# Graph and expert layer on one core: row statistics moved to ScalarE, a spread tile built on ScalarE, 448 tiles sorted and 336 scattered

## The reference, cut to what matters

```
h   = layernorm(x)                            # no weights, eps 1e-5
in_ = segment_mean((h @ W_in.T + b_in)[src], dst)
out = segment_mean((h @ W_out.T + b_out)[dst], src)
gi  = concat(in_, out) @ W_ih.T + b_ih;  gh = h @ W_hh.T + b_hh
r, z = sigmoid(i_r + h_r), sigmoid(i_i + h_i);  n = tanh(i_n + r * h_n)
x   = x + (1 - z) * h + z * n
x   = x + mixture(layernorm(x))               # 6 experts, top 2, three layers each
```

## Time and profile before

| | us |
|---|---|
| median of 3 runs | 3228.31 (3223.29 to 3228.78) |
| the profiled execution | 3225.96 |
| its span | 3224.2 |
| busy in the span: PE / VectorE / ScalarE / POOL | 2485.8 / 2135.0 / 836.3 / 2275.8 |
| POOL's scatters L390, 384 | 392.9 |
| POOL's gathers L423, 784 + 784 | 787.5 + 771.8 |

### The profile page before, as it was taken

The page is one execution under the profiler, slowest core; times in us unless marked ns, Lnnn a source line. Parts: engine busy times, 40 slices in busy tenths (PEclk is TensorE's granted clock), DMA queues, the critical chain, the costliest instruction groups (busy, mean ns, idle before and its releaser), DMA issues. The chain is left out here.

```text
span 3224.2 us, 68778 instructions
## 1 busy us (share of the span) xinstructions
PE 2485.8 (77%) x14180; PEld 1527.8 (47%) x14181; DVE 2135.0 (66%) x7172; ACT 836.3 (26%) x1328; POOL 2275.8 (71%) x2224
## 2 busy tenths in 40 slices
PE   4506699948888888788885888888888888488885
PEld 2202355524444444444442555555555555377774
DVE  8878999757777777777773666666666766622221
ACT  0030366512222222222220111111111111144443
POOL 3177777767777777777775777777777776167785
PEclk9957999979999999999997999999989999699998
DMA  2040000043333333333332444444444444135454
GB/s 77 17 122 9 1 1 0 0 142 107 109 109 109 107 107 107 102 103 107 106 107 83 128 127 128 127 127 129 128 127 124 134 125 119 34 66 79 78 80 53
DMA packets 167884, 293.80 MB, mean 91 GB/s; under 512 B 46611, under 2 KB 112916, under 8 KB 167830
## 3 DMA queue, kind: packets, MB, share of 16 engines
q0 software_dynamic: 109056, 235.68, 28.6%
q10 hardware_dynamic: 38566, 36.42, 3.4%
q1 hardware_dynamic: 20208, 21.15, 2.1%
HBM read 250.60 MB, written 42.49 MB: 91 GB/s over the span
## 5 line engine op out<-in xcount | busy, mean ns | idle before, releaser
L423 POOL DMA_INDIRECT ring<-split_rows,live x784 | 787.5, 1004 | 250.7 <-issue 234.6
L423 POOL DMA_INDIRECT over<-split_rows,gather_row x784 | 771.8, 984 | 238.7 <-issue 234.1
L1564 PE MATMUL bank<-over,over 128*128 (+1 forms) x4728 | 862.2, 334 | 10.4 <-DVE over L961 5.3
L1564 PEld LDWEIGHTS bank<-over,over 128*128 (+1 forms) x4728 | 455.9, 98 | 351.7 <-issue 122.9
L390 POOL DMA_INDIRECT list<-sort,sort x384 | 392.9, 1023 | 238.8 <-issue 124.9
L1638 PE MATMUL bank<-over,dense 128*128 x980 | 291.6, 399 | 150.3 <-SPq L518 75.9
L957 DVE TENSOR_SCALAR over<-iota_cols,live,live 128x128 f16 x1564 | 394.9, 317 | 1.0 <-issue 0.7
L1638 PE MATMUL bank<-ring,dense 128*128 x980 | 284.8, 392 | 115.2 <-issue 66.9
L1639 PE MATMUL bank<-ones_col,dense 128*128 128x1 f16 x1960 | 330.6, 169 | 0.0
L578 ACT ACTIVATE over<-live,live 128x788 f16 x245 | 222.2, 946 | 322.3 <-PE bank L1564 186.4
L1638 PEld LDWEIGHTS bank<-over,dense 128*128 x980 | 98.4, 100 | 313.6 <-issue 231.3
(11 more groups left out here) (296 smaller groups left out, 3674.6 us busy)
## 6 DMA issues: line engine op xcount, KB each, us to landing
ring<-split_rows,live POOLq DMA_INDIRECT x784
over<-split_rows,gather_row POOLq DMA_INDIRECT x784, 2.8
dense<-in_x ACTq DMA_DIRECT2D x52, 128.0 KB
dense<-in_edge_means ACTq DMA_DIRECT2D x52, 128.0 KB
routed_rows<-dense ACTq DMA_DIRECT2D x25, 264.0 KB
norm<-in_x SPq DMA_DIRECT2D x10, 640.0 KB, 5.6
split_rows<-norm SPq DMA_DIRECT2D x10, 640.0 KB, 4.0
in_edge_means<-dense ACTq DMA_DIRECT2D x50, 128.0 KB
```

Source lines behind the costliest of these rows:

```text
L423: g.indirect_dma_start(out=rings[d][:, i % ring_slots[d], :], out_offset=None, in_=table[:], in_offset=bass.IndirectOffsetOnAxis(ap=gather ...
L1564: ins = t.matmul(bank[h][:, 0:HS + 1], rows_(half), slots(h), start=False, stop=False, skip_group_check=True)
```

## The change

- **Sizes.** 448 tiles are sorted instead of 400, so that 336 are scattered.
- **Statistics on ScalarE.** ScalarE sums each row with an accumulating Identity (scale -1/256) and its squared distances with an accumulating Square, group by group, while VectorE runs `positions(0)`. SP loads x a first time for that, right behind the edges.
- **One chain for all tiles.** `row_scales` on VectorE computes all inverse roots at once, on 51 columns, and from them `rstd_plus`, `rstd_big`, `mean_scaled` and `mean_big`; the kernel before made two of these at the border to direction 1.
- **Rows on ScalarE.** SP loads x a second time; ScalarE makes rows times 2048 with one Identity a tile and rounds them. VectorE subtracts (`low_rows`), straight into fp16, within `positions(1)`: five groups after counting groups 4, 6, 8, 10, 12 and five after pairs of buckets 1, 3, 5, 7, 9. The scaling pass of ScalarE (L558) is gone. The high half is now 2048 times as large and the low half unscaled, so the mean uses one factor `1 / (2048 count)`, and one multiplication a bucket is gone.
- **Spread tile.** POOL makes it with one column per bucket; ScalarE copies it out to 128 columns each. `iota_half` is made by VectorE.
- **Order.** The fold's bias products come first and PE waits for their copy only; the weights' copies are waited for after the counting of direction 1. The loops of `positions` on VectorE are written out, and their increments of `turn` are gone. Several buffers lie elsewhere.

```diff
-SORTED_TILES = 400
+SORTED_TILES = 448
+COUNT_LOW = (4, 6, 8, 10, 12)
+PLACE_LOW = (1, 3, 5, 7, 9)
...
-            g.memset(spread_row, 0.0).then_inc(S["spread_ready"], 1)
+            g.memset(spread_base[:], 0.0).then_inc(S["spread_ready"], 1)
...
+            for s_ in range(2, LN_GROUPS):
+                sp.wait_ge(S["ln_stats"], s_ - 1)
+                sp.dma_start(ln_x[s_ % 2], x_b[s_]).then_inc(ln_in[s_ % 2], 16)
             for k in range(2):
+                sp.wait_ge(S["ln_stats"], LN_GROUPS - 1 + k)
                 sp.dma_start(ln_x[k], x_b[k]).then_inc(ln_in[k], 16)
+            for s_ in range(LN_GROUPS):
+                if s_ + 2 < LN_GROUPS:
+                    sp.wait_ge(S["h_ready"], s_ + 1)
+                    sp.dma_start(ln_x[s_ % 2], x_b[s_ + 2]).then_inc(ln_in[s_ % 2], 16)
+                sp.wait_ge(S["split_ready"], s_ + 1)
+                sp.dma_start(table_b[s_], ln_split[s_ % 2]).then_inc(store_landed[s_ % 2], 16)
+                sp.wait_ge(store_landed[s_ % 2], (s_ // 2 + 1) * 16)
+                sp.sem_inc(S["table_stored"], 1)
...
+            act.wait_ge(S["spread_ready"], 3)
+            a.copy(spread_row, spread_base[:].rearrange("p (b o) -> p b o", o=1).to_broadcast([P, NB, P])
+                   ).then_inc(S["spread_ready"], 1)
+            def ln_sums(s_):
+                k = s_ % 2
+                act.wait_ge(ln_in[k], (s_ // 2 + 1) * 16)
+                for t_ in range(LB):
+                    col = s_ * LB + t_
+                    ins = a.activation(ln_h[k][:, t_, :], ln_x[k][:, t_, :], ACT.Identity, scale=-1.0 / D,
+                                       accum_out=neg_mean[:, col:col + 1])
+                ins.then_inc(S["ln_mean"], 1)
+                act.wait_ge(S["ln_mean"], s_ + 1)
+                for t_ in range(LB):
+                    col = s_ * LB + t_
+                    ins = a.activation(ln_h[k][:, t_, :], ln_x[k][:, t_, :], ACT.Square, bias=neg_mean[:, col:col + 1],
+                                       accum_out=square_sum[:, col:col + 1])
+                ins.then_inc(S["ln_stats"], 1)
+            def ln_rows(s_):
+                k = s_ % 2
+                act.wait_ge(ln_in[k], (LN_GROUPS // 2 + s_ // 2 + 1) * 16)
+                if s_ >= 2:
+                    act.wait_ge(S["table_stored"], s_ - 1)
+                for t_ in range(LB):
+                    col = s_ * LB + t_
+                    ins = a.activation(ln_h[k][:, t_, :], ln_x[k][:, t_, :], ACT.Identity,
+                                       scale=rstd_big[:, col:col + 1], bias=mean_big[:, col:col + 1])
+                ins.then_inc(S["h_ready"], 1)
+                act.wait_ge(S["h_ready"], s_ + 1)
+                a.copy(ln_split[k][:, :, 0:D], ln_h[k]).then_inc(S["hi_ready"], 1)
...
+            def row_scales():
+                v.wait_ge(S["ln_stats"], LN_GROUPS)
+                inverse_root(step, rstd[:], square_sum[:], root_a[:], root_b[:], D)
+                e.tensor_scalar(rstd_plus[:], rstd[:], 1.0, None, ALU.add)
+                e.tensor_scalar(rstd_big[:], rstd[:], LO_SCALE, None, ALU.mult)
+                step(e.tensor_tensor(mean_scaled[:], neg_mean[:], rstd[:], ALU.mult))
+                e.tensor_scalar(mean_big[:], mean_scaled[:], LO_SCALE, None, ALU.mult).then_inc(S["rows_scaled"], 1)
+            def low_rows(s_):
+                k = s_ % 2
+                v.wait_ge(S["hi_ready"], s_ + 1)
+                e.tensor_tensor(ln_split[k][:, :, D:2 * D], ln_h[k], ln_split[k][:, :, 0:D], ALU.subtract
+                                ).then_inc(S["split_ready"], 1)
...
+                    e.tensor_scalar(iota_half, iota_cols[:], -0.5, None, ALU.add).then_inc(S["half_ready"], 1)
...
             positions(0)
-            layer_norm()
+            row_scales()
             positions(1)
```

More of the change, by code:

```diff
@@ L164, in gnn_moe_program @@
         raw_list = list_at
+        late = at["live"]
         step_gap = carve("live", [NS])
@@ L180, in gnn_moe_program @@
         at["norm"] = at["sort"]
-        assert at["sort"] <= LIVE - sort_words
         ln_x = [carve("norm", [LB, D]) for _ in range(2)]
[L183 to L189, removed]
+        assert at["norm"] <= LIVE - sort_words
+        late_at = region_at + 4 * late
+        ln_h = [over(late_at + 4 * k * LB * D, [LB, D]) for k in range(2)]
+        ln_split = [over(late_at + 4 * (2 + k) * LB * D, [LB, 2 * D], F16) for k in range(2)]
+        assert late + 4 * LB * D <= at["live"]
         gather_row = [gather_row_0, sb("gather_row_1", [P, NS], I32)]
         receiver = [receiver_0, sb("receiver_1", [P, NS], F32)]
-        moments = sb("moments", [P, NB + 1, 2], F32)
-        rstd = sb("rstd", [P, NB + 1], F32)
+        neg_mean, square_sum, rstd, rstd_plus, rstd_big, mean_scaled, mean_big, root_a, root_b = [
+            sb(n, [P, NB + 1], F32) for n in ("neg_mean", "square_sum", "rstd", "rstd_plus", "rstd_big", "mean_scaled",
+                                              "mean_big", "root_a", "root_b")]
+        spread_base = sb("spread_base", [P, NB], F16)
         ring_at = -(-nc.sbuf_base // 32) * 32
@@ L465, in _ @@
             sp.dma_start(key, edges).then_inc(S["edges_in"], 16)
+            x_b = x[0:NP, :].rearrange("(s t p) d -> s p t d", t=LB, p=P)
+            table_b = table.rearrange("(s t p) d -> s p t d", t=LB, p=P)
+            for k in range(2):
+                sp.dma_start(ln_x[k], x_b[k]).then_inc(ln_in[k], 16)
             sp.wait_ge(S["consts"], N_CONSTS)
@@ L561, in _ @@
+            for s_ in range(LN_GROUPS):
+                ln_sums(s_)
             act.wait_ge(S["fold_summed"], 1)
+            a.copy(gate_bias[0:2, 0:2 * D], banks[0][0:2, 0:2 * D])
+            a.copy(gate_bias[0:2, 2 * D:G3], banks[1][0:2, 0:D]).then_inc(S["bias_folded"], 1)
+            act.wait_ge(S["fold_summed"], 2)
             for m in range(4):
-                a.copy(w_gate[:, m, 0:2 * D], banks[m][:, 0:2 * D])
-                a.copy(w_gate[:, m, 2 * D:G3], banks[4 + m // 2][:, m % 2 * D:m % 2 * D + D])
@@ L565, in _ @@
-            a.copy(gate_bias[0:2, 0:2 * D], banks[6][0:2, 0:2 * D])
-            a.copy(gate_bias[0:2, 2 * D:G3], banks[7][0:2, 0:D]).then_inc(S["fold_done"], 1)
+                a.copy(w_gate[:, m, 0:2 * D], banks[2 + m][:, 0:2 * D])
+                ins = a.copy(w_gate[:, m, 2 * D:G3], banks[6 + m // 2][:, m % 2 * D:m % 2 * D + D])
+            ins.then_inc(S["fold_done"], 1)
+            act.wait_ge(S["rows_scaled"], 1)
+            for s_ in range(LN_GROUPS):
+                ln_rows(s_)
             def hi_mean_step(q, k):
@@ L873, in onehot @@
                                     ).then_inc(S["onehot_ready"], 1)
-                with v.Fori(0, COUNT_GROUPS // 2) as r:
-                    for g_ in range(2):
-                        v.wait_ge(S["onehot_used"], r * 2 + (u0 + g_ + 1))
-                        for k in range(GROUP):
-                            i = g_ * GROUP + k
-                            onehot(bass.ds(r * (2 * GROUP) + i, 1), i, iota_down)
-                v.wait_ge(S["onehot_used"], u0 + COUNT_GROUPS)
-                for b in range(COUNT_GROUPS // 2 * 2 * GROUP, NB):
-                    onehot(slice(b, b + 1), b % (2 * GROUP), iota_down)
+                for g_ in range(COUNT_GROUPS):
+                    v.wait_ge(S["onehot_used"], u0 + g_ + 1)
+                    for b in range(g_ * GROUP, min(g_ * GROUP + GROUP, NB)):
+                        onehot(slice(b, b + 1), b % (2 * GROUP), iota_down)
+                    if d == 1 and g_ in COUNT_LOW:
+                        low_rows(COUNT_LOW.index(g_))
                 v.wait_ge(S["onehot_used"], u0 + COUNT_GROUPS + 2)
@@ L1502, in fold_weights @@
                                        start=(n_ == 0), stop=(n_ == 3))
+                ins.then_inc(S["fold_summed"], 1)
+                for m in range(4):
+                    a_, c = m // 2, m % 2
+                    for o, lo_, hi_ in ((banks[2 + m][:, 0:2 * D], 0, 2 * D),
+                                        (banks[6 + m // 2][:, m % 2 * D:m % 2 * D + D], 2 * D, G3)):
+                        for k in range(2):
+                            ins = t.matmul(o, w_conv[:, 2 * a_ + k, c * P:c * P + P], w_ih_raw[:, 2 * a_ + k, lo_:hi_],
+                                           start=(k == 0), stop=(k == 1))
                 ins.then_inc(S["fold_summed"], 1)
```

148 lines of the change are left out of this document (34 added, 114 removed).

## The result

| | before | changed |
|---|---|---|
| median, us | 3228.55 (4 runs, 3223.29 to 3236.39) | 3135.11 (4 runs, 3125.23 to 3139.17) |
| ratio | | 0.9704, 95% interval 0.9674 to 0.9734 |
| profiled execution / its span | 3225.96 / 3224.2 | 3125.23 / 3123.1 |
| first scatter / decoding starts | 141.38 / 663.55 | 114.50 / 571.96 |
| PE's last step of the sort begins | 636.16 | 554.62 |

The forecast was 3147 in 3132 to 3165.

The account below looks back on a forecast made before the run. POOL's scatter chain was taken to bound the start of the gathers. Scatters starting 17.9 us earlier (16.4 - 0.5 + 2) and 48 fewer of them bring the decoding 79 us earlier: 3225.96 - 79 = 3147 us, range 3132 to 3165.

Parts of the forecast that it names:

- What bounds: Before the gathers, POOL's scatter chain is later than VectorE's and PE's by 26 us; through the gathers, POOL's issue rate.
- (1) Spread tile: At the start of POOL's chain, moving the wide spread tile off POOL frees VectorE's first operations: net 16.4 us.
- (2) Unrolled place loop: In the list positions before the first scatter, writing out the loop and dropping empty increments saves 2 us (0 to 4).
- (3) Scatters: On POOL up to the decoding, 48 scatters fewer; the remaining ones take 456.1 us, 1.358 each.
- VectorE's and PE's chain: Positions, row scales and sort: PE ends at 572.0, staying ahead of the decoding at 584.0.
- The new wait: In the second positions, VectorE waits for ScalarE's high parts: 4.6 us in the counting, none in the placing.
- rival with 10.1 us a group: High part, subtraction, store and load take 10.1 us a group, VectorE's chain ends last: 3166 us, chance 0.14.
- Sums on ScalarE: Row sums and squares beside the first positions take about 55 us, done near 75, hidden before row scales at 123.7.
- the rival: Sums late: accumulated form doubles each activation and table sets switch, sums end at 150 to 160: 3165 us, chance 0.05.
- The rest: Dropped multiplication per bucket and other small moves give 0; nothing after the first gather changes, 2560.7 us from decoding to end.
- POOL faster: Rival: scatters take 1.31 us each, POOL ends at 563.5 and PE's 572.0 decides: 3134 us, chance 0.13.

Follow-up runs that it names:

- e3: Changed kernel with the spread tile made by POOL over all 6400 columns again, without ScalarE's copy: 4527.36 us, ratio to before 0.9807.
- e5: Kernel before with VectorE's loops of `positions` written out, increments of `turn` kept: 4609.65 us beside 4659.48 of before, first scatter at 139.07.
- e6: Kernel before with VectorE's loops of `positions` written out and the increments of `turn` removed: 4641.5 us beside 4659.48 of before.
- e7: Changed kernel once more, no edit: 3132.38 us beside 3233.1 of the kernel before.
- e8: Kernel before with 448 tiles sorted instead of 400, on chip 1: 4646.67 us, ratio to before 0.9931.
- e12: Changed kernel with 464 tiles sorted and all ten subtractions in the placing, on chip 13: 4549.31 us, ratio to before 0.9737.
- e1: Kernel before with 448 tiles sorted instead of 400, on chip 15: 4577.81 us, ratio to before 0.9931.
- e2: Changed kernel with 400 tiles sorted instead of 448, on chip 15: 4517.24 us, ratio to before 0.9796.
- e4: Changed kernel with 464 tiles sorted instead of 448, on chip 15: 4474.46 us, ratio to before 0.9724.
- e9: Changed kernel with 400 tiles sorted instead of 448, on chip 1: 4557.83 us, ratio to before 0.9751.
- e10: Changed kernel with 464 tiles sorted instead of 448, on chip 1: 4544.06 us, ratio to before 0.9722.

## Why the prediction was right, point by point

- **What bounds.** Right. POOL's chain ended last before and does after. Behind it POOL still idles 0.3 us between gathers, and PE holds up 23 of those of direction 1 for 7.0 us in all, where it was 15 for 4.6.
- **(1) Spread tile.** 16.4 us predicted, 16.5 to 16.7 in e3. Right. The early loads of x, put at 0.5, cost nothing: the head starts at 6.00 us, where it started at 6.21.
- **(2) Unrolled place loop.** The step that failed, by its size: 2 us (0 to 4), measured 2.3 for the loops and 7.3 for the increments. I counted two increments a pair where there are three, and took the written-out part of the earlier trace rows, 3.01 us a pair, as the price of a pair without a loop, though it still had the increments. The sum at the start is 26.9 instead of 17.9.
- **(3) Scatters.** 456.1 us predicted at 1.358 each, 453.0 measured at 1.348. Right; the shift of the decoding was 91.6 for 79.6, and of the 12.0 between them 9.0 lie at the start and 3.0 here.
- **VectorE's and PE's chain.** Row scales 3.5 us for 4. The second positions took 131.3 us (118.16 to 249.4) for 138.5. Their place loop took 68.6 us without its subtractions, where it had taken 78.0 before: the same loops and increments again, 9.3 us where the sum had 2. Against that stand waits of 10.0 us (8.1 and 1.9, below), where it had 5.1. The sort to PE's end 304.7 us for 305.4. PE's last step came at 554.62 for 572.0, and its slack was 17.3 us, where the prediction's own 584.0 and 572.0 leave 12.0 (it says 12.2).
- **The new wait.** Right in its place, larger in size than the sum had it. The subtractions of the changed kernel and what VectorE waited for ahead of them:

```profile
135.46 1.49 DVE L841 TENSOR_TENSOR over<-over,over 128x1280 f16<-128x1280 f32 x1 [1.15 <-ACT over L570]
...
158.30 1.49 DVE L841 TENSOR_TENSOR over<-over,over 128x1280 f16<-128x1280 f32 x1 [3.28 <-ACT over L570]
```

  The five in the counting cost 8.1 us in all for 4.6 predicted, the five in the placing nothing. SP's ring brings a group every 6.8 to 7.1 us, not 5.4. PE's fold took 17.5 us for 17.4, from 110.98 on, and VectorE's masks then waited 1.9 us for PE, where I had 0.5 (0 to 5). The rival with 10.1 us a group is refuted.
- **Sums on ScalarE.** Hidden. They end at 66.9 us for 75. ScalarE's groups in the first 80 us of the changed kernel (count, busy, mean ns, idle before):

```profile
L555 ACT ACTIVATE over<-norm,neg_mean 128x256 f32<-128x256 f32 x50 | 24.7, 496 | 0.3
L549 ACT ACTIVATE over<-norm 128x256 f32<-128x256 f32 x50 | 20.0, 401 | 0.0
L555 ACT ACTIVATION_READ_ACCUMULATOR over<-norm,neg_mean 128x1 f32 x50 | 9.3, 187 | 0.0
L549 ACT ACTIVATION_READ_ACCUMULATOR over<-norm 128x1 f32 x50 | 9.3, 186 | 0.0
L541 ACT COPY sort<-spread_base 128x6400 f16<-128x6400 f16 x1 | 5.5, 5524 | 0.0
L541 ACT ACT_TABLE_LOAD x1 | 1.3, 1283 | 13.9 <-issue 13.9
```

  The accumulated form is a second instruction of 0.19 us that lies mostly beside its neighbours: the groups' busy times make 63.3 us, and the hundred tiles took 46.1, from 20.76 on. There is one table load, ahead of the first copy, and none between Identity and Square: the 20 loads that the prediction reckoned by the Trainium skill ("ScalarE: Activation LUTs", section "Table sets: the hidden batching unit") didn't come, since the two functions were served by one table here, and the rival is refuted. (20 times the prediction's 2.66 us are 53, not 54.) The kernel before has five such loads: one at 12.65 us and then one in every round of ScalarE's loop over pairs of groups but the first, 20.2 us apart, although both operations in it are copies. The changed kernel has no such loop, and one load. The spread copy took 5.52 us for 6.3.
- **The rest.** 2560.7 us from decoding to end, 2551.1 and 2557.6 measured: a difference of 3 to 10 us that the spread of the runs covers.

The median came out 12 us below the forecast, as much as the decoding was early. The forecast proper, 3139 to 3155 with a chance of 0.60, was missed by 4 us; the time lies in the whole range because "POOL faster" had set its lower end. That rival named 3134, the right size, for a reason that didn't hold: the scatters took 1.348 us, not 1.31, and PE didn't decide. So the path and two of its three terms were right, and that the number fell inside the range is in part luck. Most of the 12 us came from the place loop.

## What to carry to other kernels

Where two chains meet at one wait, set the size that moves work between them only after the chain that will be late has been shortened, and work out the crossing from each chain's price per unit (here 1.348 us a scatter against 0.682 us a sorted tile). In a loop of dependent instructions on VectorE, count the bare semaphore increments (0.1 us each here); they have no rows of their own, and part of them hides in the time of a group of two. POOL work over wide tiles at the start of a kernel is not free beside VectorE, even where nothing waits for its result.

## What the runs showed of the hardware

- A bare semaphore increment in VectorE's chain cost 0.1 us (7.3 us for 75, e5 to e6).
- **A pace 1.44 times slower, cause open.** The kernel before took 4608 to 4678 us on chips 15, 6, 1 and 13, where other runs took 3228 and 3233; chip 1 gave both paces (e7, e8). Up to the first scatter the traces agree to 1.5 us. Busy time of the engines in stretches of e7 (window, length, then PE, PE's loads, VectorE, ScalarE and POOL with counts, clock, DMA share, GB/s):

```profile
5.00:115.00 110.00, 62.68 (x314) 30.39 (x315) 102.47 (x189) 52.63 (x202) 2.00 (x13) 0.95 0.33 107
115.00:250.00 135.00, 73.40 (x352) 35.42 (x351) 121.50 (x220) 46.22 (x76) 104.71 (x100) 0.91 0.30 88
250.00:400.00 150.00, 150.00 (x885) 86.28 (x884) 145.80 (x578) 99.88 (x113) 112.89 (x113) 0.99 0.02 1
```

  and of e12:

```profile
5.00:115.00 110.00, 63.06 (x309) 30.62 (x310) 101.67 (x188) 52.55 (x202) 2.01 (x13) 0.94 0.35 107
115.00:250.00 135.00, 34.19 (x112) 14.74 (x109) 22.91 (x61) 11.41 (x22) 102.17 (x106) 0.61 0.03 5
250.00:400.00 150.00, 13.08 (x40) 4.62 (x39) 9.36 (x24) 0.00 (x0) 111.92 (x117) 0.50 0.02 1
650.00:940.00 290.00, 289.95 (x1726) 167.19 (x1724) 268.72 (x1061) 188.23 (x210) 0.00 (x0) 1.00 0.00 0
```

  While POOL scatters, POOL keeps its pace and VectorE and PE all but stand; once it stops, they run at full pace again. Yet scatters alone don't do it. In e5 and e6, as slow in the end, the normalisation ran beside them at the normal pace: between 142 and 243 us VectorE was busy 79.9 us in e5 and 29.8 in e1, and the long waits of e5 and e6 begin near 250 us, in the second positions. Nor is it the list alone: from the decoding to the end e1 took 3557 us, where 2561 are normal, so most of the time is lost behind the decoding. Beside the scatters of e12, VectorE's groups of masks come 22.4 us apart:

```profile
201.79 1.42 DVE L868 TENSOR_SCALAR over<-sort,sort 128x784 f16<-128x784 f16 x4 [20.75 <-remote]
...
224.19 1.48 DVE L868 TENSOR_SCALAR over<-sort,sort 128x784 f16<-128x784 f16 x4 [20.98 <-issue]
```

  The instructions themselves are as long as ever (four masks 1.42 us); what grows is the wait between them. In e1 even VectorE's waits on itself take 1.23 us in the normalisation (0.03 at the normal pace, and in e5):

```profile
185.74 0.17 DVE L812 SCALAR_TENSOR_TENSOR norm<-norm,norm 128x5 f32<-128x5 f32 x1 [1.23 <-DVE norm L811]
```

  So at the slow pace VectorE's and PE's work starts in earnest when the scatters end, and the decoding comes some 340 to 430 us after them; in the changed kernel that makes fewer scatters pay (e2 to e4 33.5 us at the decoding, e9 to e10 29.9). For the 0.7% of e1 and e8 it isn't shown: e5, the kernel before with 400 tiles and written-out loops, decodes at 999.8, ahead of e1's 1018.2. Why a chip runs so, and why chip 1 did once and once not, no run here shows.
